# Second layer of a fused transformer kernel: the last bias as a one-row product on TensorE, the 8-bit rounding scale in one operation less

## The chip, the cores and the metric

The kernel runs on one core of a Trainium2 chip. The metric is the device time of one execution in microseconds (us), as the median of several runs. Three runs of the kernel before gave 1072.55, 1074.01 and 1078.31 us.

## The reference, cut to what matters

Sixteen batches of 256 tokens with 256 features pass through attention, a mixture of experts, a second attention, and a last linear layer whose input and weight are first rounded to a small grid in blocks of 32:

```python
x = x + xattn0(layernorm(x), ctx)             # 16 heads, 120 context rows
x = x + experts(layernorm(x))                 # 8 experts, two per token
x = x + xattn1(layernorm(x), ctx, ctx, mask)  # one head of 256
x = x + ffn1(layernorm(x), weight, bias)      # below

def ffn1(x, weight, bias):
    s = max(max|block of 32| / 7.5, 1e-30)    # one scale per block
    xd = nearest(x / s, fp6 grid) * s         # the weight in the same way, as wd
    return xd @ wd.T + bias
```

The change touches only the last line of the model: its bias, its residual and the scale of its blocks.

## The kernel before, in words

All five engines run one program after the other: attention, routing, experts and the second phase (`second_phase`), which holds the last two lines of the model. The order on each engine is written out by hand, with semaphores between engines; each engine takes its instructions strictly in that order.

The second phase handles one batch (two tiles of 128 tokens, `[128, 2, 256]` in float32) at a time. `CYCLES` runs from -2 to 17, and in cycle c each engine works at up to four batches: statistics of the experts' sum for batch c+2, layer norm and scores of batch c+1, softmax and attention of batch c, and rounding and last linear layer of batch c-1. Cycles -1 to 2 also project the context of two more batches each (`project_context`) on TensorE.

The steps that the prediction names, with their lines:

- VectorE: `attended` (L1773) adds the attention to the residual, which gives x4. `scales` (L1755, L1758, L1761, L1762) takes the maximum of each block of the normalised x4, makes the scale `sc` from it, writes `sc * 64` over the maxima in `am` (64 is one over FP8_DOWN), and takes the reciprocal of `sc`.
- GpSimd: `add_bias` (L1675) writes x4 plus the bias row `fb` (which stands in all 128 partitions) into `x4b`. `to_blocks` (L1683) multiplies the normalised x4 by the reciprocal scale; `scale_back` (L1690) multiplies the rounded 8-bit values by `am`. `inverse_std` makes the inverse deviations of the three norms by a power.
- ScalarE: `normalise` (L1804) writes the normalised x3 and x4, `exps` (L1840) the softmax, `round_blocks` (L1853) rounds by writing 8-bit floats, with FP8_DOWN as its scale, and `keep_xdT` (L1859), `keep_result` (L1864) and others copy results out of PSUM.
- TensorE: `turn_probs` (L1964), `weigh` (L1972), `turn_rows` (L1929), `start_result` (L1903: the identity times `x4b` into `f_ps`), `scores` (L1956), `turn_quantised` (L1896) and `linear` (L1911, which adds the last layer to `f_ps`), in this order in each cycle.

In the profile a float32 product of up to 512 columns appears as two MATMUL instructions.

Of the kernel before, what the change touches and what calls it, by code (L numbers as in the profile page):

```python
# [22 lines left out]
ALU = mybir.AluOpType  # L23
# [3 lines left out]
P = 128  # L27
# [15 lines left out]
QMAX = 7.5  # L43
TINY = 1e-30
# [4 lines left out]
FP8_DOWN = 2.0 ** -6  # L49
# [13 lines left out]
def ge(eng, sem, value):  # L63

    if isinstance(value, int) and value <= 0:
        return
    eng.wait_ge(sem, value)
# [13 lines left out]
def build(nc, x, ctx, mask, wq0, wkv0, w1, b1, w2, b2, gate_w, shared_w, shared_b, gamma, beta,  # L81
# [10 lines left out]
    with outer:  # L92
# [47 lines left out]
        rows.close()  # L140
        weights.close()
        last = second_phase(nc, sem, past, ident, second, x2_d, acc_d, ctx, out)

        with nc.Block() as block:
# [1330 lines left out]
def second_phase(nc, sem, past, ident, second, x2_d, acc_d, ctx, out):  # L1475
# [7 lines left out]
    with st:  # L1483
        def sb(name, shape, dt=F32):
            return st.enter_context(nc.sbuf_tensor(name, shape, dt))

        def ps(name, shape, dt=F32):
            return st.enter_context(nc.psum_tensor(name, shape, dt))

        T2 = [P, 2, D]  # L1490
        CTX_RING = 8
        wv, wkq, wdT, gam, fb, bound, half = (
            second[k] for k in ("wv", "wkq", "wdT", "gam", "fb", "bound", "half"))

        def ring(name, shape, dt=F32, n=RING):
            return [sb(f"{name}{i}", shape, dt) for i in range(n)]
# [9 lines left out]
        nmax, psum_, rs = (ring("c_nmax", [P, 2], n=2), ring("c_prob_sum", [P, 2], n=2),  # L1506
                           ring("c_rs", [P, 2], n=2))
        pT = ring("c_probsT", [P, 2, P], n=2)
        x4, xn4, x4b = ring("c_x4_", T2, n=2), ring("c_xn4_", T2, n=2), ring("c_x4b", T2, n=2)
        am, sc, rsc = (ring("c_amax", [P, 2 * NB], n=2), ring("c_scale", [P, 2 * NB], n=2),  # L1510
                       ring("c_rscale", [P, 2 * NB], n=2))
        vq, q8 = ring("c_vq", T2, n=2), ring("c_q8_", T2, FP8, n=2)
        xd, xdT = ring("c_xd", T2, n=2), ring("c_xdT", [P, 2, KC, P], n=2)
        o = ring("c_out", T2, n=2)
        tie = sb("c_tie", [P, 1])

        class Norm:

# [34 lines left out]
        f_ps = ps("c_f_ps", T2)  # L1553
# [4 lines left out]
        s_tie = sem("c_tie_set")  # L1558
# [18 lines left out]
        s_rs = sem("c_rs_ready")  # L1577
        s_x4 = sem("c_x4_ready")
        s_xn4 = sem("c_xn4_ready")
        s_x4b = sem("c_x4_bias")  # L1580
        s_am = sem("c_amax_ready")
        s_sc = sem("c_scale_ready")
        s_rsc = sem("c_rscale_ready")
        s_vq = sem("c_vq_ready")
        s_q8 = sem("c_q8_ready")
# [3 lines left out]
        s_f_p = sem("c_ffn_psum")  # L1589
# [3 lines left out]
        def exists(n):  # L1593
            return 0 <= n < B

        def blocks(a):
            return a[:].rearrange("p u (g c) -> p (u g) c", c=BLK)

        def per_block(a):
            return a[:].unsqueeze(2).broadcast_to([P, 2 * NB, BLK])  # L1600
# [55 lines left out]
        def gpsimd(pool):  # L1656
            def inverse_std(g, n):
                i = n % 2
                pool.wait_ge(g.s_st, g.variance(n))
                pool.tensor_scalar(g.ve[i][:], g.mv[i][:, :, 1], g.eps, None, ALU.add  # L1660
                                   ).then_inc(g.s_r, 1)
                if g is not NA:
                    pool.tensor_scalar(g.nm[i][:], g.mv[i][:, :, 0], -1.0, None, ALU.mult)
                pool.wait_ge(g.s_r, g.inverse(n) - 1)
                pool.tensor_tensor(g.rstd[i][:], g.ve[i][:], half[:], ALU.pow
                                   ).then_inc(g.s_r, 1)
                if g is not NA:
                    pool.wait_ge(g.s_r, g.inverse(n))
                    pool.tensor_tensor(g.nb[i][:], g.nm[i][:], g.rstd[i][:], ALU.mult  # L1669
                                       ).then_inc(g.s_r, 1)  # L1670

            def add_bias(n):
                pool.wait_ge(s_x4, n + 1)
                ge(pool, s_f_p, n - 1)
                pool.tensor_tensor(x4b[n % 2][:], x4[n % 2][:],  # L1675
                                   fb[:].unsqueeze(1).broadcast_to(T2), ALU.add
                                   ).then_inc(s_x4b, 1)

            def to_blocks(n):
                pool.wait_ge(s_rsc, n + 1)  # L1680
                pool.wait_ge(s_xn4, n + 1)
                ge(pool, s_q8, n - 1)
                pool.tensor_tensor(blocks(vq[n % 2]), blocks(xn4[n % 2]), per_block(rsc[n % 2]),  # L1683
                                   ALU.mult).then_inc(s_vq, 1)

            def scale_back(n):
                pool.wait_ge(s_q8, n + 1)
                pool.wait_ge(s_rsc, n + 1)
                ge(pool, s_xdT_p, n - 1)
                pool.tensor_tensor(blocks(xd[n % 2]), blocks(q8[n % 2]), per_block(am[n % 2]),  # L1690
                                   ALU.mult).then_inc(s_xd, 1)

            for s, value in past["experts"]:
                pool.wait_ge(s, value)
            pool.memset(tie[:], TIE * FP8_DOWN).then_inc(s_tie, 1)
            for c in CYCLES:
                if exists(c + 1):
                    inverse_std(N3, c + 1)
                if exists(c - 1):
                    add_bias(c - 1)  # L1700
                    to_blocks(c - 1)
                if exists(c + 2):
                    inverse_std(NA, c + 2)
                if exists(c - 1):
                    scale_back(c - 1)
                if exists(c):
                    inverse_std(N4, c)

        def vector(dve):
# [41 lines left out]
            def scales(n):  # L1751
                i = n % 2
                dve.wait_ge(s_xn4, n + 1)
                ge(dve, s_xd, n - 1)
                dve.tensor_reduce(am[i][:], blocks(xn4[i]), AX.X, ALU.max,  # L1755
                                  apply_absolute_value=True).then_inc(s_am, 1)
                dve.wait_ge(s_am, n + 1)
                dve.tensor_scalar(sc[i][:], am[i][:], 1.0 / QMAX, TINY, ALU.mult, ALU.max  # L1758
                                  ).then_inc(s_sc, 1)
                dve.wait_ge(s_sc, n + 1)  # L1760
                dve.tensor_scalar(am[i][:], sc[i][:], 1.0 / FP8_DOWN, None, ALU.mult)  # L1761
                dve.reciprocal(rsc[i][:], sc[i][:]).then_inc(s_rsc, 1)  # L1762

            def attended(n):
                i = n % 2
                dve.wait_ge(s_e, n + 1)
                dve.reciprocal(rs[i][:], psum_[i][:]).then_inc(s_rs, 1)
                dve.wait_ge(s_rs, n + 1)
                dve.wait_ge(s_o_p, n + 1)
                ge(dve, s_x4b, n - 1)  # L1770
                ge(dve, s_xn4, n - 1)
                for u in range(2):
                    j = dve.scalar_tensor_tensor(out=x4[i][:, u, :], in0=o_ps[:, u, :],  # L1773
                                                 scalar=rs[i][:, u:u + 1], in1=x3[n % RING][:, u, :],
                                                 op0=ALU.mult, op1=ALU.add)
                j.then_inc(s_x4, 1)

            dve.wait_ge(second["s_vec"], 32)
            for c in CYCLES:
# [4 lines left out]
                if exists(c + 2):  # L1784
                    n = c + 2
# [7 lines left out]
                if exists(c + 2):  # L1793
                    n = c + 2
# [4 lines left out]
        def scalar(act):  # L1799
# [50 lines left out]
            def round_blocks(n):  # L1850
                act.wait_ge(s_vq, n + 1)
                ge(act, s_xd, n - 1)
                act.activation(q8[n % 2][:], vq[n % 2][:], ACT.Identity, bias=tie[:],  # L1853
                               scale=FP8_DOWN, saturate=False).then_inc(s_q8, 1)

            def keep_xdT(n):
                act.wait_ge(s_xdT_p, n + 1)
# [32 lines left out]
        def tensor(pe):  # L1890
# [7 lines left out]
                j.then_inc(s_xdT_p, 1)  # L1898

            def start_result(n):  # L1900
                pe.wait_ge(s_x4b, n + 1)
                ge(pe, s_o, n)
                pe.matmul(f_ps[:].rearrange("p u d -> p (u d)"), ident[:],  # L1903
                          x4b[n % 2][:].rearrange("p u d -> p (u d)"),
                          start=True, stop=False, skip_group_check=True)

            def linear(n):
                pe.wait_ge(s_xdT, n + 1)
                for u in range(2):
                    for k in range(KC):  # L1910
                        j = pe.matmul(f_ps[:, u, :], xdT[n % 2][:, u, k, :], wdT[:, k, :],  # L1911
                                      start=False, stop=(k == KC - 1), skip_group_check=True)
                j.then_inc(s_f_p, 1)
# [67 lines left out]
            for c in CYCLES:  # L1981
# [11 lines left out]
                if exists(c - 1):  # L1993
                    turn_quantised(c - 1)
                    linear(c - 1)

        return Programs(sync, gpsimd, tensor, vector, scalar)


# [21 lines left out]
```

## Time and profile before

| | |
|---|---|
| median of 3 runs | 1074.01 us |
| the profiled execution | 1070.92 us |
| its span, first to last instruction | 1069.1 us |
| TensorE busy | 945.4 us, 88% |
| VectorE busy | 560.1 us, 52% |
| ScalarE busy | 497.1 us, 46% |
| GpSimd busy | 539.3 us, 50% |
| granted TensorE clock, mean | 0.962 |
| second phase | from about 880 us to the end |

Busy shares are means over very different phases. The change lies in the last 190 us alone, so the rows below are from there. A row of the timeline gives the start, the duration from the first start to the last end, the engine, the line, the operation with output and inputs, and how many instructions were merged. In brackets stands how long the engine was idle before it and who released it. Instructions of one engine overlap by some tens of ns, so distances are best taken from start to start.

### The profile page before, as it was taken

The numbers are of one execution on the slowest core, as the hardware profiler recorded it, in microseconds if no ns is written. First come the engines' busy times: TensorE is split into PE (matmuls) and PEld (weight loads), VectorE is DVE, ScalarE is ACT, GpSimd is POOL, SyncE is SP. The second block draws the span as 40 slices with busy tenths as digits, with TensorE's granted clock in tenths as the row PEclk, the third lists the DMA queues.
The fourth block names the chain that finished last, engine by engine and source line by source line (L and its number), as shares of the span: only waits on it lengthen the run. The fifth ranks groups of instructions, "written<-read, shape, count | busy, mean of one in ns | idle before, by whom it ended". The sixth has DMA issues, their size and how long they took to land.

```text
span 1069.1 us, 21031 instructions
## 1 busy us (share of the span) xinstructions
PE 945.4 (88%) x7159; PEld 808.6 (76%) x7159; DVE 560.1 (52%) x1231; ACT 497.1 (46%) x1257; POOL 539.3 (50%) x654
## 2 busy tenths in 40 slices
PE   6999999999823699999999999999999989787776
PEld 4777777777612699999999999999999978554544
DVE  3888888888769223433223223322322313679882
ACT  3666666666642233333333333333333324666663
POOL 2333333333325455555565565555556532578883
PEclk9999999999955799999999999999999998999998
DMA  5434343433217521222221221222222244122201
GB/s 142 142 111 152 100 153 101 156 103 135 80 22 203 148 41 30 41 37 35 41 40 31 41 40 32 40 40 33 39 41 36 35 91 118 43 76 90 90 33 35
DMA packets 74709, 80.11 MB, mean 75 GB/s; under 512 B 12752, under 2 KB 69904, under 8 KB 74480
## 3 DMA queue, kind: packets, MB, share of 16 engines
q1 hardware_dynamic: 58704, 60.12, 18.6%
q0 software_dynamic: 15904, 18.66, 11.1%
q8 instruction: 61, 1.00, 0.4%
q14 instruction: 40, 0.33, 0.1%
HBM read 52.51 MB, written 26.25 MB: 74 GB/s over the span
## 4 chain that ended last, share of the span: by engine, by line
PE 60%; DVE 20%; issue 8%; POOL 6%; ACT 5%; DMA 2%; POOLq 0%; SPq 0%; DVEq 0%; ACTq 0%
PE b_H L1269 24%; PE b_Y L1281 23%; DVE a_max L635 5%; DVE a_probs L641 4%; PE a_T L506 2%; ACT a_probs L738 2%; PE a_S L496 2%; PE b_xT L1256 1%; PE c_g_ps L1940 1%; PE c_v_ps L1945 1%; POOL a_rstd L401 1%; PE c_f_ps L1911 1%; DVE a_xin L625 1%; ACT c_xn L1804 1%; DVE c_x L1773 1%
## 5 line engine op out<-in xcount | busy, mean ns | idle before, releaser
L1435 ACT ACTIVATE b_hiddenT<-b_H,b_b 128x128 f32<-128x128 f32 x568 | 162.4, 368 | 331.9 <-PE b_H L1269 331.9
L1269 PEld LDWEIGHTS b_H<-b_rowsT,b_w 128*128 128x128 f32 x2272 | 266.6, 193 | 6.0 <-ACT b_rowsT L1444 2.4
L1269 PE MATMUL b_H<-b_rowsT,b_w 128*128 128x128 f32 x2272 | 267.3, 276 | 1.8 <-ACT b_rowsT L1444 1.8
L1281 PE MATMUL b_Y<-w_sb,b_hiddenT 128*128 x1136 | 256.8, 379 | 0.0
L1227 POOL DMA_INDIRECT ffn_rows<-b_y,scatter_idx x71 | 154.0, 2169 | 193.7 <-DVE b_y L1360 185.2
L1281 PEld LDWEIGHTS b_Y<-w_sb,b_hiddenT 128*128 128x128 f32 x1136 | 210.5, 190 | 25.7
L1356 DVE TENSOR_TENSOR b_y<-b_Y,b_bc 128x256 f32<-128x256 f32 x71 | 30.2, 425 | 324.1 <-PE b_Y L1281 324.1
L1349 DVE COPY b_w<-w_sb 128x2048 f32 x71 | 87.1, 1227 | 37.5 <-issue 26.0
L635 DVE TENSOR_REDUCE a_max<-a_S 128x8 f32<-128x960 f32 x64 | 73.6, 1149 | 26.9 <-PE a_S L496 25.1
L1213 POOL DMA_INDIRECT b_rows<-xn_rows,gather_idx x71 | 73.5, 1035 | 21.5 <-issue 19.7
L744 ACT COPY a_probsT<-a_T 120x512 f32<-120x512 f32 x128 | 69.1, 594 | 28.1 <-PE a_T L506 28.1
L1219 POOL DMA_INDIRECT b_weight<-choice_weights,slot_idx x71 | 67.4, 950 | 21.6 <-issue 21.6
L506 PE MATMUL a_T<-ident,a_probs 128*120 128x128 f32 x512 | 68.5, 277 | 10.6 <-ACT a_probs L738 8.3
L641 DVE TENSOR_TENSOR a_probs<-a_S,a_max 128x960 f32<-128x960 f32 x64 | 74.1, 1157 | 2.2
L738 ACT ACTIVATE a_probs<-a_probs 128x960 f32<-128x960 f32 x64 | 64.7, 1011 | 22.0 <-DVE a_probs L641 21.3
L506 PEld LDWEIGHTS a_T<-ident,a_probs 128*120 128x120 f32 x512 | 55.1, 137 | 22.8 <-ACT a_probs L738 16.9
L413 POOL TENSOR_TENSOR a_x<-a_x,a_xres 128x256 f32<-128x256 f32 x32 | 23.3, 729 | 84.9 <-DVE a_x L652 84.9
L1911 PE MATMUL c_f_ps<-c_wdT,c_xdT 128*128 128x256 f32 x128 | 33.7, 408 | 10.8 <-ACT c_xdT L1859 10.8
L513 PE MATMUL a_O<-a_probsT,a_vaug 120*32 120x128 f32 x1024 | 41.8, 279 | 1.0 <-ACT a_probsT L744 0.9
L513 PEld LDWEIGHTS a_O<-a_probsT,a_vaug 120*32 120x32 f32 x1024 | 23.9, 109 | 22.2 <-issue 11.5
L405 POOL TENSOR_SCALAR a_var_eps<-a_mv 128x1 f32<-128x1 f32 x32 | 7.0, 220 | 65.4 <-DVE a_mv L661 65.4
L1804 ACT ACTIVATE c_xn<-c_x,c_x_nb,c_x_rstd 128x256 f32<-128x256 f32 x64 | 35.0, 597 | 9.9 <-POOL c_x_nb L1669 9.9
(219 smaller groups left out, 1367.2 us busy)
## 6 DMA issues: line engine op xcount, KB each, us to landing
w_sb<-in_L_ffn_W SPq DMA_DIRECT2D x32, 512.0 KB, 4.5
a_xin<-in_x SPq DMA_DIRECT2D x16, 256.0 KB, 3.0
a_xres<-in_x SPq DMA_DIRECT2D x32, 128.0 KB, 2.0
xn_rows<-a_xn SPq DMA_DIRECT2D x32, 128.0 KB, 2.3
x_rows<-a_x SPq DMA_DIRECT2D x32, 128.0 KB, 2.0
ffn_rows<-shared SPq DMA_DIRECT2D x2, 2048.0 KB, 18.6
c_x<-x_rows SPq DMA_DIRECT2D x16, 256.0 KB, 2.7
c_acc<-ffn_rows SPq DMA_DIRECT2D x16, 256.0 KB, 2.7
```

The costliest lines, as they stand in the source:

```text
L506: i = pe.transpose(T_ps[q % 2][0:CTX, j * P:(j + 1) * P], pr[q // 2][:, 4 * (q % 2) + j, :], ident[:])
L635: dve.tensor_reduce(mx[h][:].rearrange("p (r j) -> p r j", r=RG), scores_of(h), AX.X, ALU.max).then_inc(s_mx, 1)
L641: dve.tensor_tensor(pr[h][:].rearrange("p (r j) c -> p r j c", r=RG), scores_of(h), mx[h][:].rearrange("p (r j) -> p r j", r=RG).unsqueeze ...
L738: act.activation(pr[h][:], pr[h][:], ACT.Exp, scale=DH ** -0.5).then_inc(s_exp, 1)
L744: act.copy(pT[q % 2][0:CTX].rearrange("p j n -> p (j n)"), T_ps[q % 2][0:CTX, :]).then_inc(s_T, 1)
L1213: pool.indirect_dma_start(xg[n % AHEAD][:], None, xn2_d, IndirectOffsetOnAxis(gather_idx[:, n:n + 1], 0)).then_inc(s_x[n % AHEAD], 16)
L1219: pool.indirect_dma_start(wt[n % AHEAD][:], None, w_d, IndirectOffsetOnAxis(slot_idx[:, n:n + 1], 0)).then_inc(s_wt[n % AHEAD], 16)
L1227: pool.indirect_dma_start(acc_d, IndirectOffsetOnAxis(scatter_idx[:, n:n + 1], 0), y[i][:], None, bounds_check=TOK + P - 1, oob_is_err=Tru ...
L1269: j = pe.matmul(H_ps[i][:, c * P:(c + 1) * P], w1c[i][:, k * HID + c * P:k * HID + (c + 1) * P], xT[:, k * P:(k + 1) * P], start=(k == 0), ...
L1281: j = pe.matmul(y_ps[i][:, 0:D], hT[i][:, c * P:(c + 1) * P], w2_sb[:, bass.ds(e * (HB * D) + c * D, D)], start=(c == 0), stop=(c == HB - 1))
L1349: dve.tensor_copy(w1c[i][:], w1_sb[:, bass.ds(e * (KC * HID), KC * HID)])
L1435: j = act.activation(hT[i][:, c * P:(c + 1) * P], H_ps[i][:, c * P:(c + 1) * P], ACT.Gelu, bias=b1c[i][:, c:c + 1])
```

## The change

The bias leaves GpSimd: `add_bias`, its tile `x4b` and its semaphore are gone. `start_result` now multiplies the identity by x4 itself, and two products (one for each tile of 128 tokens) of a row of ones `[1, 128]` by the bias row `[1, 256]` add the bias to `f_ps`. The row of ones is set once by GpSimd. VectorE, which writes x4 two cycles later into the same buffer, waits for the linear layer instead of for `add_bias`.

The scale is made in the 8-bit range at once: `sc` now holds what `am` held (64 times the old scale), its reciprocal holds FP8_DOWN already, so `round_blocks` has no scale, `scale_back` reads `sc`, and the multiplication L1761 is gone.

```diff
-            def add_bias(n):
-                pool.wait_ge(s_x4, n + 1)
-                ge(pool, s_f_p, n - 1)
-                pool.tensor_tensor(x4b[n % 2][:], x4[n % 2][:],
-                                   fb[:].unsqueeze(1).broadcast_to(T2), ALU.add
-                                   ).then_inc(s_x4b, 1)
...
-                pool.tensor_tensor(blocks(xd[n % 2]), blocks(q8[n % 2]), per_block(am[n % 2]),
+                pool.tensor_tensor(blocks(xd[n % 2]), blocks(q8[n % 2]), per_block(sc[n % 2]),
                                    ALU.mult).then_inc(s_xd, 1)
...
             pool.memset(tie[:], TIE * FP8_DOWN).then_inc(s_tie, 1)
+            pool.memset(one[:], 1.0).then_inc(s_tie, 1)
             for c in CYCLES:
...
                 if exists(c - 1):
-                    add_bias(c - 1)
                     to_blocks(c - 1)
...
-                dve.tensor_scalar(sc[i][:], am[i][:], 1.0 / QMAX, TINY, ALU.mult, ALU.max
-                                  ).then_inc(s_sc, 1)
+
+                dve.tensor_scalar(sc[i][:], am[i][:], 1.0 / QMAX / FP8_DOWN, TINY / FP8_DOWN,
+                                  ALU.mult, ALU.max).then_inc(s_sc, 1)
                 dve.wait_ge(s_sc, n + 1)
-                dve.tensor_scalar(am[i][:], sc[i][:], 1.0 / FP8_DOWN, None, ALU.mult)
                 dve.reciprocal(rsc[i][:], sc[i][:]).then_inc(s_rsc, 1)
...
-                ge(dve, s_x4b, n - 1)
+                ge(dve, s_f_p, n - 1)
...
                 act.activation(q8[n % 2][:], vq[n % 2][:], ACT.Identity, bias=tie[:],
-                               scale=FP8_DOWN, saturate=False).then_inc(s_q8, 1)
+                               saturate=False).then_inc(s_q8, 1)
...
             def start_result(n):
-                pe.wait_ge(s_x4b, n + 1)
+                pe.wait_ge(s_x4, n + 1)
+                pe.wait_ge(s_tie, 2)
                 ge(pe, s_o, n)
                 pe.matmul(f_ps[:].rearrange("p u d -> p (u d)"), ident[:],
-                          x4b[n % 2][:].rearrange("p u d -> p (u d)"),
+                          x4[n % 2][:].rearrange("p u d -> p (u d)"),
                           start=True, stop=False, skip_group_check=True)
+                for u in range(2):
+                    pe.matmul(f_ps[:, u, :], one[:], fb[0:1, :], start=False, stop=False,
+                              skip_group_check=True)
```

## Rows read from the trace of the kernel before

**Rows 1.** Windows: length, busy time (instructions) of each engine, granted clock, DMA share, GB/s.
```profile
945.00:990.00 45.00, 33.63 (x167) 22.47 (x166) 41.02 (x128) 29.15 (x68) 37.08 (x67) 1.00 0.31 94
```

**Rows 2.** Timeline of VectorE, from one x4 to the next.
```profile
963.15 0.88 DVE L1773 SCALAR_TENSOR_TENSOR c_x<-c_o_ps,c_rs,c_x 128x256 f32<-128x256 f32 x2
...
968.11 0.69 DVE L1755 TENSOR_REDUCE c_amax<-c_xn 128x16 f32<-128x512 f32 x1 [0.44 <-ACT c_xn L1804]
968.83 0.91 DVE L1758 TENSOR_SCALAR c_scale<-c_amax 128x16 f32<-128x16 f32 x1
969.77 0.18 DVE L1761 TENSOR_SCALAR c_amax<-c_scale 128x16 f32<-128x16 f32 x1
969.86 0.25 DVE L1762 RECIPROCAL c_rscale<-c_scale 128x16 f32<-128x16 f32 x1
...
972.02 0.88 DVE L1773 SCALAR_TENSOR_TENSOR c_x<-c_o_ps,c_rs,c_x 128x256 f32<-128x256 f32 x2
```

**Rows 3.** Timeline of GpSimd in the same cycle.
```profile
968.44 1.26 POOL L1675 TENSOR_TENSOR c_x4b<-c_x,c_fb 128x512 f32<-128x512 f32 x1
```

**Rows 4.** L1758 over all batches (ns min/median/max), and timeline rows of a later cycle.
```profile
L1758 DVE TENSOR_SCALAR c_scale<-c_amax x16: 174/908/914, 920.3 to 1056.7; 128x16 f32<-128x16 f32 x16
1003.90 1.27 POOL L1675 TENSOR_TENSOR c_x4b<-c_x,c_fb 128x512 f32<-128x512 f32 x1
1004.71 0.49 DVE L1758 TENSOR_SCALAR c_scale<-c_amax 128x16 f32<-128x16 f32 x1
```

**Rows 5.** Timeline of ScalarE, cycles 2 to 4.
```profile
940.65 0.59 ACT L1859 COPY c_xdT<-c_xdT_ps 128x512 f32<-128x512 f32 x1
941.13 1.09 ACT L1804 ACTIVATE c_xn<-c_x,c_x_nb,c_x_rstd 128x256 f32<-128x256 f32 x2
...
948.40 0.59 ACT L1859 COPY c_xdT<-c_xdT_ps 128x512 f32<-128x512 f32 x1 [1.70 <-PE c_xdT_ps L1896]
949.25 1.09 ACT L1804 ACTIVATE c_xn<-c_x,c_x_nb,c_x_rstd 128x256 f32<-128x256 f32 x2 [0.26 <-POOL c_x_nb L1669]
...
958.12 1.09 ACT L1804 ACTIVATE c_xn<-c_x,c_x_nb,c_x_rstd 128x256 f32<-128x256 f32 x2 [1.02 <-POOL c_x_nb L1669]
```

**Rows 6.** Timeline of TensorE, between the two copies of L1859 above.
```profile
941.29 1.99 PE L1911 MATMUL c_f_ps<-c_wdT,c_xdT 128*128 128x256 f32 x8 [0.68 <-ACT c_xdT L1859]
943.12 0.38 PE L1964 MATMUL c_zp_ps<-ident,c_probs 128*120 128x128 f32 x2
...
945.43 0.66 PE L1929 MATMUL c_xnT_ps<-ident,c_xn 128*128 128x128 f32 x4 [0.34 <-ACT c_xn L1804]
945.92 1.02 PE L1903 MATMUL c_f_ps<-c_x4b,ident 128*128 128x512 f32 x2
...
947.77 0.60 PE L1896 MATMUL c_xdT_ps<-ident,c_xd 128*128 128x128 f32 x4
```

**Rows 7.** TensorE's weight loads of the linear layer (ns min/median/max).
```profile
L1911 PEld LDWEIGHTS c_f_ps<-c_wdT,c_xdT x128: 186/190/338, 929.8 to 1064.8; 128*128 128x128 f32 x128
```

**Rows 8.** Timeline of TensorE, first cycle with a start of the result.
```profile
922.76 1.02 PE L1903 MATMUL c_f_ps<-c_x4b,ident 128*128 128x512 f32 x2
```

**Rows 9.** Timeline of TensorE, where the granted clock is at its lower level.
```profile
995.47 0.43 PE L1964 MATMUL c_zp_ps<-ident,c_probs 128*120 128x128 f32 x2 [0.87 <-ACT c_probs L1840]
...
997.84 1.05 PE L1929 MATMUL c_xnT_ps<-ident,c_xn 128*128 128x128 f32 x4 [0.34 <-ACT c_xn L1804]
...
1001.75 0.60 PE L1896 MATMUL c_xdT_ps<-ident,c_xd 128*128 128x128 f32 x4
...
1062.07 3.78 PE L1911 MATMUL c_f_ps<-c_wdT,c_xdT 128*128 128x256 f32 x8 [0.68 <-ACT c_xdT L1859]
```

**Rows 10.** Timeline of three engines near the end.
```profile
1047.19 1.09 ACT L1804 ACTIVATE c_xn<-c_x,c_x_nb,c_x_rstd 128x256 f32<-128x256 f32 x2
1051.24 0.88 DVE L1773 SCALAR_TENSOR_TENSOR c_x<-c_o_ps,c_rs,c_x 128x256 f32<-128x256 f32 x2 [1.65 <-issue]
1060.28 1.11 PE L1896 MATMUL c_xdT_ps<-ident,c_xd 128*128 128x128 f32 x4 [2.46 <-POOL c_xd L1690]
```

More of the change, by code:

```diff
@@ L1508, in second_phase @@
         pT = ring("c_probsT", [P, 2, P], n=2)
-        x4, xn4, x4b = ring("c_x4_", T2, n=2), ring("c_xn4_", T2, n=2), ring("c_x4b", T2, n=2)
+        x4, xn4 = ring("c_x4_", T2, n=2), ring("c_xn4_", T2, n=2)
         am, sc, rsc = (ring("c_amax", [P, 2 * NB], n=2), ring("c_scale", [P, 2 * NB], n=2),
@@ L1515, in second_phase @@
         tie = sb("c_tie", [P, 1])
+        one = sb("c_one", [1, P])
         class Norm:
@@ L1579, in second_phase @@
         s_xn4 = sem("c_xn4_ready")
-        s_x4b = sem("c_x4_bias")
         s_am = sem("c_amax_ready")
```

## The prediction, as put on record before the change was built

> **What bounds the kernel now.** I read the page first (which engine is busy where), then the chain of waits over the last 200 us, then the timeline of each engine over single cycles, and last the tiles and lines that the change touches. The page says TensorE is busy 88% of the span, but that is the experts. In the chain the second phase falls into three stretches: up to about 946 us the chain runs through TensorE's projections of the contexts; from 946 to 1042 us it goes round VectorE, GpSimd and ScalarE and hardly touches TensorE; the last 20 us are a chain through every engine. In the middle stretch VectorE is busy 41.0 of 45 us, GpSimd 37.1, TensorE 33.6, at full granted clock [rows 1].
>
> The middle stretch repeats every 972.02 - 963.15 = 8.87 us [rows 2]. Two rings run in it side by side.
>
> Ring A sets the 8.87: VectorE makes x4 and its statistics, GpSimd the inverse deviation, ScalarE the normalised x4, on which VectorE waits 0.44 us at L1755; then maximum, scale, reciprocal, the statistics and centring of a later batch, and the next x4 [rows 2]. A thing to see in it: L1758 works on 16 columns and takes 0.91 us. Its least is 0.174 [rows 4]. In the steady cycle it ends at 969.74, and `add_bias` on GpSimd ends at 968.44 + 1.26 = 969.70 [rows 2, 3]. One cycle has it started later, at 1004.71: it ends at 1005.20, `add_bias` at 1005.17, and it takes 0.49 [rows 4]. So L1758 does not run while `add_bias` does, and ends 0.03 to 0.04 after it.
>
> Ring B is TensorE and ScalarE: linear layer, `turn_probs`, attention, normalised x3 (ScalarE), `turn_rows`, `start_result`, `scores`, `turn_quantised`, and `keep_xdT` (L1859) on ScalarE, behind which the normalised x4 and the next linear layer stand in their queues. Where it is alone on the path it takes 948.40 - 940.65 = 7.75 us from copy to copy [rows 5], without a gap between linear layer and `turn_probs` [rows 6]. In the steady cycle it has room: ScalarE waits 1.02 us for GpSimd before it normalises x4 [rows 5], and TensorE 0.87 us before `turn_probs` [rows 9].
>
> **The change, part by part.**
>
> *`add_bias` goes, on ring A.* Its small norm operations were done when `add_bias` started at 968.44, so GpSimd is idle when L1758 starts, and L1758 takes 0.17 instead of 0.91: -0.74 us in each steady cycle. GpSimd's next step, `to_blocks`, needs the reciprocal and moves with it.
>
> *L1761 goes, on ring A.* The reciprocal starts 969.86 - 969.77 = 0.09 earlier [rows 2]: -0.09. Ring A becomes 8.87 - 0.74 - 0.09 = 8.04 us. The lost scale of L1853 and another input of L1690 have the same sizes: nothing.
>
> *Two products are added, on ring B.* They are four MATMUL instructions of 256 columns, right behind `start_result` and in front of `scores`. The trace has no product with a one-row contraction. The nearest row is the linear layer, with the same columns into the same PSUM tile: 943.12 - 941.29 = 1.83 us for eight, 0.229 each [rows 6], so 0.92 for four. Bound from below: as many instructions of 128 columns take 945.92 - 945.43 = 0.49 [rows 6]; less than none is excluded, since instructions are only added to TensorE. From above: if no weight load hid behind a product, 4 x 0.19 more [rows 7], 1.68. I take 0.92, the row with the same shape.
>
> The one row is the point at which the change invites a wrong price: 1/128 of the multiplications. The Trainium skill (TensorE: Matmul & The Clock Gate, Step-by-step: what each phase is for) says of the weight load that its time goes by columns and that the row count does not matter, and its section Why this matters for your kernels gives a 32-row product the time of a 128-row one. By it the four cost what a full product does, my 0.92; no row here has few rows, so the trace neither confirms nor denies it.
>
> Ring B becomes 7.75 + 0.92 = 8.67 us, longer than ring A's 8.04. So the binding ring changes: ScalarE reaches the normalised x4 late, behind `keep_xdT`, which waits for TensorE. A cycle gains 8.87 - 8.67 = 0.20 us, not 0.83.
>
> *Waits.* TensorE's wait for the row of ones is met from the start. Its wait is now for x4 instead of x4 plus bias, earlier and never last in a steady cycle. VectorE's wait for the linear layer of two batches back is behind `weigh` in TensorE's order, for which it waits anyway; nothing. The memset of the ones comes once, on GpSimd at the start of the phase, where GpSimd waits for its first statistics: hidden; uncovered it would count once, not per cycle.
>
> **The sum**, in the profiled execution's time, batch by batch:
>
> 1. Cycles 1 and 2 are bound by TensorE without idle at `start_result` [rows 8]: 2 x 0.92 = +1.84, and nothing is gained, as L1758 already takes 0.17 there.
> 2. Cycle 3: the copy at 948.40 moves by 1.84 + 0.92 to 951.16; the normalised x4 follows 941.13 - 940.65 = 0.48 behind, at 951.64, against 949.25 [rows 5]: +2.39. GpSimd is no longer the last (it was, by 0.26; TensorE moved by 0.92 more than it).
> 3. From there 11 rings of 8.67 to the normalised x4 of batch 14: 951.64 + 95.37 = 1047.01. It was at 1047.19 [rows 10]. (8.87 times 11 would be 97.6; the old one lost another 0.4 there, as the clock was low.)
> 4. x4 of batch 15 follows 1051.24 - 1047.19 = 4.05 later [rows 10]: at 1051.06, -0.18. The last batch then runs alone through all engines; there `add_bias` and the four products lie beside waits (TensorE idles 2.46 us before `turn_quantised` [rows 10]), and only L1761 counts: -0.09.
>
> In all -0.27 us: the span from 1069.1 to 1068.8, the execution from 1070.92 to 1070.65. The profiled execution is 3.1 us under the median and under the lowest of the three runs shown, so I apply the difference to the median: 1074.01 - 0.27 = 1073.7 us.
>
> The sum hangs on one price: the four products are on the path 2 + 1 + 11 = 14 times, so every 0.1 us on them is 1.4 us.
>
> **The rivals.**
>
> *R1, the products are nearly free.* At the lower bound of 0.49 ring B is 8.24. Steps as above: 948.40 + 3 x 0.49 + 0.48 = 950.35; plus 11 x 8.24 = 1040.99; plus 4.05 = 1045.04, which is -6.20, and -0.09: 1074.01 - 6.3 = 1067.7, faster by 0.6%. For it: one row of work. Against it: the columns are 256 each, and the 256-column row is 0.229 [rows 6]. Chance 0.10.
>
> *R2, slower: the weight loads of the one-row products show.* TensorE changes between a 128-row and a one-row operand and back in every cycle; if the four loads do not hide, the price is 1.68, and the 0.76 counts 14 times: +10.6, 1084.4 us. It passes +0.5% (5.4 us) from a price of 0.92 + 5.6 / 14 = 1.32 on. For it: no row shows this change of form. Against it: in the linear layer eight loads of 0.19 lie beside eight products of 0.229 and nothing shows. Chance 0.10.
>
> *R3, the low clock falls on ring B.* The old trace has a stretch where `turn_rows` to `turn_quantised` takes 1001.75 - 997.84 = 3.91 instead of 947.77 - 945.43 = 2.34 us [rows 6, 9]; ring B had 1.0 us of room, so it cost little. Now it would cost 1.57, and 0.92 for the products at half clock: 2.5 each. Two of them give 1074.01 - 0.3 + 5.0 = 1078.7. For it: it happens in the old trace after a cycle with 0.87 us of idle before `turn_probs` and little work after. Against it: in the new ring that idle is filled, and cycles of that form (941 to 948) kept the full clock. Chance 0.08, most of it within 0.5%.
>
> *R4, the clock holds in the last batch.* The linear layer there takes 3.78 at the low level instead of 1.99, its transposes 1.11 instead of 0.60 [rows 6, 9, 10]: up to 2.3 less, 1071.4. The products shorten the idle in front of it. The Trainium skill (TensorE: Matmul & The Clock Gate, What's actually happening) has activity release the throttle, which speaks for this. Chance 0.12, within 0.5%.
>
> *R5, the change doesn't free L1758.* If something else stretches it, ring A is 8.78 and binds: 11 x 0.11 more, 1074.9. The three agreeing ends speak against it. Chance 0.05.
>
> My forecast keeps 0.55. Its own range is 1072.5 to 1075.5 (products from 0.84 to 1.05). 0.5% of this kernel is 5.4 us, about what a measurement can tell from no change. Faster by more: R1, and R4 together with cheap products, 0.11. Slower by more: R2 and a part of R3, 0.12. Within: 0.77. The range of 8 in 10 runs from 1069.0, short of R1, to 1078.7, R3: with the 1.5 us by which a median can move either way it leaves out R1 and R2.
>
> **What would show it.** L1758 at 0.17 in all batches. Steady distance of x4 to x4 8.67 (8.04 if the products were hidden). Start of `scores` 0.92 behind the end of the identity product. No idle before `turn_probs`, ScalarE's normalised x4 released no longer by GpSimd but right behind `keep_xdT`, and VectorE idle before L1755 about 1.1 us instead of 0.44. x4 of batch 3 later by about 1.8. The prediction is wrong if the four products take under 0.55 or over 1.32, or if the chain in the middle still runs through GpSimd.

## The result, and the profile after

| | before | after |
|---|---|---|
| median (20 runs each) | 1073.62 us | 1078.03 us |
| ratio, 95% interval | | 1.0044 (1.003 to 1.0059) |
| the profiled execution / its span | 1070.92 / 1069.1 us | 1077.03 / 1075.3 us |

The changed kernel is slower by 4.4 us, which the interval tells from no change. It lies inside the range of the prediction, under the bound of 0.5%, and on the other side of no change than the forecast of 1073.7, which was 0.3 us faster.

The two profiled executions' spans are 6.2 us apart, but 2.9 of these were there at the first `start_result` (922.76 before [rows 8], 925.66 after), ahead of anything the products could delay. From there to the end of the span it is 1069.1 - 922.76 = 146.3 us before and 1075.3 - 925.66 = 149.6 after: that stretch lost 3.3 us.

The changed kernel's VectorE, one steady cycle (start, duration, engine, line, operation; idle before and releaser in brackets), which answers to [rows 2]:

```profile
959.48 0.88 DVE L1766 SCALAR_TENSOR_TENSOR c_x<-c_o_ps,c_rs,c_x 128x256 f32<-128x256 f32 x2
...
965.30 0.69 DVE L1748 TENSOR_REDUCE c_amax<-c_xn 128x16 f32<-128x512 f32 x1 [1.20 <-ACT c_xn L1797]
966.02 0.18 DVE L1752 TENSOR_SCALAR c_scale<-c_amax 128x16 f32<-128x16 f32 x1
966.23 0.25 DVE L1755 RECIPROCAL c_rscale<-c_scale 128x16 f32<-128x16 f32 x1
...
968.40 0.88 DVE L1766 SCALAR_TENSOR_TENSOR c_x<-c_o_ps,c_rs,c_x 128x256 f32<-128x256 f32 x2
```

The scale operation takes 0.18 instead of 0.91 us: the gain is there. It is handed back at the maximum, which waits 1.20 us for ScalarE instead of 0.44. From x4 to x4 it is 8.92 us instead of 8.87. The timeline of its ScalarE over the same cycle, answering to [rows 5]:

```profile
954.78 0.59 ACT L1852 COPY c_xdT<-c_xdT_ps 128x512 f32<-128x512 f32 x1 [2.85 <-PE c_xdT_ps L1889]
955.26 1.09 ACT L1797 ACTIVATE c_xn<-c_x,c_x_nb,c_x_rstd 128x256 f32<-128x256 f32 x2
...
963.70 0.59 ACT L1852 COPY c_xdT<-c_xdT_ps 128x512 f32<-128x512 f32 x1 [2.85 <-PE c_xdT_ps L1889]
964.18 1.09 ACT L1797 ACTIVATE c_xn<-c_x,c_x_nb,c_x_rstd 128x256 f32<-128x256 f32 x2
```

and the timeline of its TensorE, answering to [rows 6]; the second row is the added products:

```profile
960.06 1.02 PE L1897 MATMUL c_f_ps<-c_x,ident 128*128 128x512 f32 x2
961.01 1.13 PE L1901 MATMUL c_f_ps<-c_fb,c_one 1*128 1x256 f32 x4
962.07 1.15 PE L1953 MATMUL c_zp_ps<-c_gT,c_xnT 128*128 128x120 f32 x8
963.06 0.60 PE L1889 MATMUL c_xdT_ps<-ident,c_xd 128*128 128x128 f32 x4
964.34 1.99 PE L1908 MATMUL c_f_ps<-c_wdT,c_xdT 128*128 128x256 f32 x8 [0.68 <-ACT c_xdT L1852]
966.17 0.38 PE L1961 MATMUL c_zp_ps<-ident,c_probs 128*120 128x128 f32 x2
```

Ring B went from 7.75 to 963.70 - 954.78 = 8.92 us and now binds: nothing stands between `keep_xdT` and the normalised x4, and no gap is left in front of `turn_probs` (L1961). From `start_result` to `turn_quantised` it is 963.06 - 960.06 = 3.00 us, against 947.77 - 945.92 = 1.85 before [rows 6]: 1.15 of the 1.17 us by which ring B grew.

### The profile page after: what moved, and what is told of

Read it like the earlier page. It is cut to its first block and busy times, and to the rows that moved or that the text cites. A ratio compares the mean times of both kernels' runs of the same rounds, so it can differ in the third digit from the quotient of the medians.

```text
span 1075.3 us, 21115 instructions
## 1 busy us (share of the span) xinstructions
PE 959.9 (89%) x7223; PEld 819.1 (76%) x7223; DVE 552.7 (51%) x1215; ACT 495.3 (46%) x1257; POOL 519.0 (48%) x639
## 5 line engine op out<-in xcount | busy, mean ns | idle before, releaser
L536 PE MATMUL a_M<-a_wsg,a_xn2T 128*128 128x264 f32 x128 | 37.0, 414 | 0.9 <-ACT a_xn2T L755 0.9
```

## The experiments

Medians of the kernel before differ a little from call to call (1074.28, 1071.74 and 1073.68 us), so runs are compared by their ratio to it. "Steady" is the distance from one x4 to the next in each kernel's own profile, one execution each. The edits are cut to the lines that matter (... stands for what is left out); where the operand of ones has more rows, or the products are repeated, its value is made smaller, so that the sum stays the bias.

**e1. The changed kernel without the products** (the bias is missing from its result).
```diff
-                for u in range(2):
-                    pe.matmul(f_ps[:, u, :], one[:], fb[0:1, :], start=False, stop=False,
-                              skip_group_check=True)
```


> The changed kernel without the two one-row products (the bias is left out of the result). Theory T (the added products lengthen the TensorE/ScalarE ring B from 7.75 to 8.92 us, and that is the whole loss): without them ring B is 7.75, ring A binds at 8.04, x4 to x4 8.04 us in the steady cycles, GpSimd releases the normalised x4 again, and the kernel is 9 to 10 us faster than before (11 x 0.83, and a little at the ends), ratio about 0.991. Rival V (the loss, or a third of it, comes from ahead of the second phase, where the changed kernel's profile was 2 us later): the start of the second phase stays 2 us later than before and the gain is 7 to 8 us. Rival W (ring A was never freed): 8.78 us, gain 1 us.

Measured: steady 8.04 to 8.05 us, 1064.09 us, ratio 0.9895 (0.9864 to 0.9926). Ring A binds at 8.04, the length forecast for it. Its second phase started at 886.8 us (the memset at its head), later than in all but one other profile here, against 880.2 in the profile before and 882.2 in the changed kernel's, and the gain is whole all the same: from the memset to the end it is 179.9 us, against 188.9 before. That start lies between 879.8 and 886.9 in the fourteen profiles, without order in the edits, so rival V falls.

**e2. Bias products from 128 rows.**
```diff
-        one = sb("c_one", [1, P])
+        one = sb("c_one", [P, P])
...
-            pool.memset(one[:], 1.0).then_inc(s_tie, 1)
+            pool.memset(one[:], 1.0 / P).then_inc(s_tie, 1)
...
-                    pe.matmul(f_ps[:, u, :], one[:], fb[0:1, :], start=False, stop=False,
+                    pe.matmul(f_ps[:, u, :], one[:], fb[:], start=False, stop=False,
```


> The changed kernel with the bias products made from 128 rows instead of one: a 128x128 matrix of 1/128 by the bias in all 128 partitions; same instructions, columns and place. Theory T1 (0.92 us of the price is the width, and 0.25 the change between operands of 128 rows and of one row, whose first weight loads do not hide): identity product to scores 0.89 + 0.87 to 0.92 us, ring 8.62 to 8.67, the kernel about 3.5 us faster than the changed one and within 1 us of before. Rival T2 (the 0.25 comes with any added products: their wait, their place in the queue): ring stays 8.92, no difference from the changed kernel.

Measured: steady 8.52 us, 1072.3 us, ratio 0.9981 (0.996 to 1.0002): clearly faster than the changed kernel (1.0044), and not told apart from the kernel before. The same instructions with 128 times the rows are 0.40 us per cycle cheaper. The timeline of TensorE in this kernel:

```profile
976.08 1.02 PE L1897 MATMUL c_f_ps<-c_x,ident 128*128 128x512 f32 x2
976.94 1.03 PE L1901 MATMUL c_f_ps<-c_fb,c_one 128*128 128x256 f32 x4
977.80 1.05 PE L1953 MATMUL c_zp_ps<-c_gT,c_xnT 128*128 128x120 f32 x8
978.68 0.60 PE L1889 MATMUL c_xdT_ps<-ident,c_xd 128*128 128x128 f32 x4
```

its weight loads (engine PEld) in the same cycle:

```profile
976.51 0.19 PEld L1901 LDWEIGHTS c_f_ps<-c_fb,c_one 128*128 128x128 f32 x1 [0.24 <-issue]
976.94 0.62 PEld L1901 LDWEIGHTS c_f_ps<-c_fb,c_one 128*128 128x128 f32 x3 [0.24 <-issue]
977.59 1.08 PEld L1953 LDWEIGHTS c_zp_ps<-c_gT,c_xnT 128*128 128x128 f32 x8
```

and the weight loads of the changed kernel, one cycle before that of its rows above (the products of these loads start at 952.10 and 953.15):

```profile
952.09 0.72 PEld L1901 LDWEIGHTS c_f_ps<-c_fb,c_one 1*128 1x128 f32 x4 [0.76 <-issue]
953.15 0.97 PEld L1953 LDWEIGHTS c_zp_ps<-c_gT,c_xnT 128*128 128x128 f32 x8 [0.33 <-issue]
```

With 128 rows the first load of each group starts ahead of its product, beside the product before: 976.51 for 976.94, and 977.59 for 977.80. With one row it starts only with its product (961.01 follows the identity product at 0.95 us instead of 0.86), and so does the first load of the full-height group behind. The three distances are 0.86, 0.86, 0.88 with 128 rows, and 0.95, 1.06, 0.99 with one. That makes 0.40, and an estimate from the loads' own times, 0.18 and 0.19 us for the two that start late, accounts for 0.37 of it.

**e7 and e8: where the surcharge sits.**
e7 has one product of 512 columns, two instructions instead of four:
```diff
-                for u in range(2):
...
+                pe.matmul(f_ps[:], one[:], fb[0:1, :].unsqueeze(1).broadcast_to([1, 2, D]),
+                          start=False, stop=False, skip_group_check=True)
```
e8 has four products of 256 columns, eight instructions:
```diff
-                for u in range(2):
+                for u in (0, 1, 0, 1):
...
```


> The changed kernel with one one-row product of 512 columns (the bias row read twice) instead of two of 256: two matmul instructions and two weight loads instead of four. Theory T1 (the surcharge of the one-row form, 0.40 us per cycle against 128 rows, sits where the form changes, before and behind the group): ring stays at 8.85 to 8.92 us. Rival U (each one-row instruction carries its part of the surcharge, 0.05 to 0.1 us): half of it goes, ring 8.7 us, 2.5 to 3 us faster than the changed kernel.

> The changed kernel with four one-row products of 256 columns instead of two (ones replaced by 0.5, the sum is the same): eight instructions instead of four. Theory T1 (surcharge at the change of form only): four more cost 0.86 to 0.92 us, ring 9.78 to 9.84, 14 x 0.9 = 12 to 13 us slower than the changed kernel. Rival U (each one-row instruction is slower, 0.264 us): 1.06 us more, ring 9.98, 15 us slower.

Measured: e7 steady 8.91 us, ratio 1.006 (1.0036 to 1.0083): half the instructions, the same price. e8 steady 9.78 us in its first cycles: four more one-row instructions cost 0.86, 0.215 each. So one row is not slower inside its group; the 0.40 us is at the two changes between operands of different height. Rival U falls. But e8's time was 1114.31 us, ratio 1.039: 14 x 0.86 = 12 us were expected on top of the changed kernel, and by the two ratios there were 37. That was in no theory.

**e9. The same eight instructions from 128 rows.**
```diff
...
+                for u in (0, 1, 0, 1):
+                    pe.matmul(f_ps[:, u, :], one[:], fb[:], start=False, stop=False,
```


> Eight instead of four bias instructions (four products), from 128 rows each: the partner of the run with eight one-row instructions, where the steady distance was 9.78 us and then 12 to 13.5 us with TensorE busy 40.5 of 45 us at a granted clock of 0.67. Theory C (the clock takes a one-row product for little or no activity): with 128 rows the clock stays at 1.00, steady 8.52 + 0.86 = 9.38 us throughout, 1083 to 1086 us. Rival D (it is the length of the group, or the order of long and short work in a cycle, whatever the rows): the granted clock falls to 0.7 as well, cycles of 12 us, over 1100 us.

Measured: steady 9.39 us to the end, 1083.06 us, ratio 1.0089 (1.0063 to 1.0115). The same window of both, e8 first (length; busy time of TensorE, its weight loads, VectorE, ScalarE, GpSimd; granted clock; DMA share, GB/s):

```profile
985.00:1030.00 45.00, 40.50 (x143) 28.02 (x142) 25.13 (x82) 18.50 (x46) 20.88 (x44) 0.67 0.19 60
```

and e9:

```profile
985.00:1030.00 45.00, 37.88 (x188) 28.53 (x189) 35.42 (x116) 26.62 (x65) 28.82 (x57) 1.00 0.25 77
```

Same instructions, same columns, same places: from one row the granted clock is 0.67 on a TensorE that is busy 90% of the window, from 128 rows it is 1.00. Rival D falls, and it comes out as theory C expected. The reason that C gives is not shown, though: the pair differs in the rows and also in the head starts that the one-row group loses, and no run has eight instructions from 32 or 64 rows. In e8 the low level (1.2 GHz) sets in behind the one-row group, in every cycle of this window; the linear layer of the same cycle took 3.78 us for 1.99, as the timeline of its TensorE shows:

```profile
1010.63 1.99 PE L1901 MATMUL c_f_ps<-c_fb,c_one 1*128 1x256 f32 x8
...
1014.81 3.78 PE L1908 MATMUL c_f_ps<-c_wdT,c_xdT 128*128 128x256 f32 x8 [0.68 <-ACT c_xdT L1852]
```

**e10 and e11. 32 and 64 rows.**
```diff
+        one = sb("c_one", [32, P])
...
+                    pe.matmul(f_ps[:, u, :], one[:], fb[0:32, :], start=False, stop=False,
```
e11 has 64 in both places.

> The changed kernel with the two bias products made from 32 rows (1/32 by the bias in 32 partitions). Measured so far: one row 8.92 us per steady cycle, 128 rows 8.52. Theory T1 (the surcharge of 0.40 us comes with any change between a full and a quarter-height operand): 8.92. Rival (it is special to one row): 8.52, or something between.

> As the run with 32 rows, with 64 rows. Theory T1 (any change between operands of different height): 8.92 us. Rival (above 32 rows the weight loads hide as in the context's products, which have 120 rows and show no surcharge): 8.52 us.

Measured: steady 8.91 us in both, ratios 1.0063 (1.0037 to 1.009) and 1.0052 (1.0033 to 1.0071). The surcharge is the same at 1, 32 and 64 rows, and gone at 128. It is not special to one row. Nor does every change of height bring it: the context's products from 120 rows stand between products from 128, and their first load keeps its head start, as two rows of the kernel before show, its load and its product:

```profile
936.18 0.25 PEld L1919 LDWEIGHTS c_ctxT_ps<-ident,c_ctx 120*128 120x128 f32 x2
936.29 0.37 PE L1919 MATMUL c_ctxT_ps<-ident,c_ctx 120*128 120x120 f32 x2
```

The context's products start 0.95 us behind `scores` (935.34 to 936.29), and 128-row products in the same place start 0.96 behind it (946.81 to 947.77). Where between 64 and 120 rows the surcharge ends, no run shows.

**e3, e5 and e12: what the scale edit is worth.** e3 is the kernel before with the scale edit alone; e5 is the changed kernel, and e12 is e6 below, with that edit undone. In e5 and e12 this line is back, and with it the old scales and the read of `am`:
```diff
...
+                dve.tensor_scalar(am[i][:], sc[i][:], 1.0 / FP8_DOWN, None, ALU.mult)
...
```


> The kernel before with only the scale made in one operation less; GpSimd still adds the bias. Theory T: L1758's successor is still held until the end of add_bias, only the 0.09 us of the multiplication goes: steady 8.78 us, 1.0 to 1.1 us faster than before (0.1%). Rival: the held operation was L1761 as well as L1758, or the scale edit alone frees VectorE: 8.04 us, 9 us faster.

> The changed kernel with the scale edit undone (L1761, its multiplication, is back), so only the bias edit is left. Theory T (ring B of TensorE and ScalarE binds, VectorE has 0.76 us of idle per cycle more than before): the 0.09 us hides, steady 8.92 us as in the changed kernel, within 0.3 us of it but for 0.1 us in the last batch. Rival: ring A still has a share in the path, 9.0 us and 1 us slower than the changed kernel.

> The fastest version (bias products of 128 rows between turn_quantised and the linear layer; steady 8.05 us) with the scale edit undone, so L1761 is back. Theory T (ring A binds there, so the scale edit counts there in full, while it hid in the changed kernel): steady 8.13 to 8.14 us, 1.0 to 1.1 us slower than the fastest version, 1063.5 us if that is at 1062.5. Rival (it hides here too): 8.05 us.

Measured: e3 steady 8.78 us, ratio 0.9979 (0.9958 to 0.9999); `add_bias` is still there, and L1758 still takes 0.91 us. e5 steady 8.91 us, as the changed kernel; its ratio of 1.0064 (1.0041 to 1.0087) overlaps with the changed kernel's, and does not resolve 0.1 us. e12 steady 8.12 us against 8.05, ratio 0.9924 (0.99 to 0.9947). The edit is worth 0.07 to 0.09 us per cycle where ring A binds, and nothing in the steady cycle where ring B does. Changed alone, it is a gain of about 1 us by an estimate from the steady cycles (11 x 0.09); the medians are too coarse to tell its size.

**e4 and e6. The products in TensorE's idle stretch.**
The two products are taken out of `start_result` into a step of their own, `add_bias` (on TensorE, not the step of that name on GpSimd before):
```diff
...
                 if exists(c - 1):
                     turn_quantised(c - 1)
+                    add_bias(c - 1)
                     linear(c - 1)
```


> The changed kernel with the two one-row products moved behind turn_quantised and ahead of the linear layer, where TensorE idles 0.68 us in every cycle waiting for keep_xdT. Theory T: 0.68 of the 1.06 to 1.17 us is hidden, ring B is 8.13 to 8.24 us, and the kernel is 6 to 7 us faster than before (ratio about 0.994). Rival G (the idle stretch does not take other products, since the linear layer's weight loads stand behind the one-row ones and lose their head start): ring B 8.3 to 8.5, 3 to 5 us faster.

> Both repairs at once: bias products from 128 rows, placed between turn_quantised and the linear layer. Price 0.77 us by the full-rows run, of which 0.68 us is idle time there: ring B 7.85 us, so ring A binds at 8.04 us in every steady cycle. Against the one-row products in the same place (steady 8.07 us): 0.3 us from the steady cycles and 2 x 0.3 us from cycles 1 and 2, so about 1 us faster than that, and 7.5 to 8.5 us faster than before (ratio 0.9925). Rival: the 128-row weight loads of the linear layer are held up as before, and there is no difference between the two.

Measured: e4 (one row) steady 8.07 us, 1067.54 us, ratio 0.9932 (0.9911 to 0.9952). e6 (128 rows) steady 8.05 us, 1062.54 us, ratio 0.9917 (0.9903 to 0.9931). Both are faster than both kernels; e6 has the shortest steady cycle and the lowest median of those that compute everything, though its interval overlaps with those of e4 and e12. The timeline of TensorE in e6:

```profile
971.44 0.60 PE L1889 MATMUL c_xdT_ps<-ident,c_xd 128*128 128x128 f32 x4
971.87 1.03 PE L1903 MATMUL c_f_ps<-c_fb,c_one 128*128 128x256 f32 x4
972.74 1.97 PE L1910 MATMUL c_f_ps<-c_wdT,c_xdT 128*128 128x256 f32 x8
974.78 0.43 PE L1963 MATMUL c_zp_ps<-ident,c_probs 128*120 128x128 f32 x2
```

The linear layer starts 1.30 us behind `turn_quantised`, where it started 1.28 behind it without products in between (963.06 to 964.34 above): the four products fill the wait for ScalarE's copy and cost 0.02. In e4 it starts 968.02 - 966.43 = 1.59 behind, so there the one-row products cost 0.31, less than the 0.38 to 0.49 that was expected.

## Why the prediction was wrong

**Right.** `add_bias` did hold L1758: without it that operation (L1752 in the changed kernel) takes 0.17 to 0.18 us in all batches, with it and the scale edit alone still 0.91 (e3), and without the products the steady cycle is 8.04 us (e1). L1761 is 0.09 us where its ring binds (e3). The binding ring changes as forecast: no idle before `turn_probs`, ScalarE no longer released by GpSimd, VectorE's idle at the maximum 1.20 us (forecast 1.1). The waits and the memset cost nothing: the one-row memset lies beside its sibling, and GpSimd then waits 5.9 us. The ring without products, 7.75 us, was read rightly: from `start_result` to `turn_quantised` the products added 1.15 us, and the ring grew by 1.17 over it.

**Wrong: the price of the added products.** The step that failed is "I take 0.92, the row with the same shape". Measured in ring B it is 8.92 - 7.75 = 1.17 us. The row had the same columns and the same destination, but its neighbours had its own height; ours do not. Made from 128 rows the same products are cheaper than I said, 0.77 us (e2: 8.52 - 7.75). The group takes 0.86 itself, and the distance from `scores` to `turn_quantised` behind it is 0.88 where it was 0.96 without the group. The two changes of height add 0.40. R2 had named this mechanism, weight loads that show, and put it at 0.76 and a chance of 0.10; what shows is the first load at each change, not all four.

The sum multiplies it by 14, and (1.17 - 0.92) x 14 = 3.5 us. The forecast of -0.3 becomes +3.2, and from the first `start_result` on the profile lost 3.3. So it is a size, not the frame, and the size turned the sign: with 0.92 the change breaks even, and everything above it is loss. That the measured time lies inside the range is luck: its upper end, 1078.7, was drawn for the low clock of R3, and the forecast's own range for the products, 0.84 to 1.05, does not hold 1.17.

**The rest of the 4.4 us.** The medians are 1.1 us further apart than the two profiles' stretches from the first `start_result` on. With the changed kernel's four products per cycle the profile shows the clock at 1.00 through the steady cycles, but its executions of 1079.0 to 1084.1 us had a mean granted clock of 0.955 to 0.960, and those of 1076.5 to 1077.2 had 0.962. No profile of one of its longer executions was kept, but one of e5 was, with the same one-row products and the same steady cycle: 1083.29 us. Its TensorE in cycle 1:

```profile
924.83 0.87 PE L1926 MATMUL c_xnT_ps<-ident,c_xn 128*128 128x128 f32 x4
925.49 1.92 PE L1897 MATMUL c_f_ps<-c_x,ident 128*128 128x512 f32 x2
927.33 2.07 PE L1901 MATMUL c_f_ps<-c_fb,c_one 1*128 1x256 f32 x4
```

A low stretch (granted clock 0.51 from 925 to 935) begins here ahead of the first bias product, behind 2.2 us in which TensorE was idle, and falls in a cycle that TensorE binds: from x4 to x4 that cycle takes 942.56 - 925.34 = 17.22 us, against 937.93 - 925.61 = 12.32 in the changed kernel's profile. So R3's mechanism does occur, 4.9 us at once in this execution. How much of the 1.1 us it makes is open: the kernel before, without one-row products, spreads over as much, 1070.5 to 1078.5 us.

**The rivals.** R1 (nearly free) had a price of 0.49, and the least seen in this place is 0.77. R3's low stretch is in the profile of e5 alone at that size. R4 did not come: the last linear layer still took 3.78 us. R5 falls with e1; the ends that spoke against it were two on record, not three.

The Trainium skill (TensorE: Matmul & The Clock Gate, Step-by-step: what each phase is for) has a weight load's time independent of the row count; that agrees with the loads here (0.18 us at one row, 0.19 at 128). Its section Why this matters for your kernels gives a 32-row product the time of a full one; that agrees for the single instruction (374 ns at 32 rows in e10, 379 at 128 in e2), but a 32-row group between 128-row ones cost 0.40 us more than a 128-row group. What the change between heights costs decided here, and it had to be measured.

## What to carry to other kernels

A product that is cheap in rows is not cheap in time: count its columns. With 1 to 64 rows between neighbours of 128, add what the first weight load on either side loses (0.40 us a cycle here); filling the operand up to 128 rows took that away. An engine with "room" has it only up to the next ring: write down the second-longest loop and its length before moving work onto it. And put added work where the engine already waits: the one-row products cost 1.17 us in front of `scores` and 0.31 behind `turn_quantised`, those from 128 rows 0.77 and 0.02.

## What the runs showed of the hardware that was not expected

- Products of 1, 32 or 64 rows between products of 128 rows lose the head start of the first weight load at each change: 0.40 us a cycle, the same for all three heights, independent of how many stand in the group (e2, e7, e8, e9, e10, e11). Products of 120 rows between products of 128 keep it (936.18 for 936.29 in the kernel before).
- With many one-row products TensorE's clock was not held as with 128-row ones: with eight instructions per cycle the granted clock was 0.67 at 90% busy, with the same eight from 128 rows 1.00, and the kernels 1114.3 and 1083.1 us (e8, e9). The busy share of an engine does not tell this; the granted clock beside it does.
